# Twenty-eight tiles of a mean edge layer looked up on TensorE from a table copy in SBUF

## The reference

```python
h = x @ W + b
agg = segment_sum(h[col], row, num_segments=n)
deg = segment_sum(ones, row, num_segments=n)
return agg * where(deg > 0, 1 / deg, 0)[:, None]
```

## Time and profile before

| | us |
|---|---|
| runs of the kernel before: median of 3 (lowest to highest) | 5398.98 (5395.08 to 5399.3) |
| the profiled execution's own time | 5395.97 |
| its span, first to last instruction | 5394.1 |
| mean granted TensorE clock of the span | 0.896 |

### The profile page before, as it was taken

The page is one execution under the profiler, slowest core; times in us unless marked ns, Lnnn a source line. Parts: engine busy times, 40 slices in busy tenths (PEclk is TensorE's granted clock), DMA queues, the critical chain, the costliest instruction groups (busy, mean ns, idle before and its releaser), DMA issues. The chain is left out here.

```text
span 5394.1 us, 106431 instructions
## 1 busy us (share of the span) xinstructions
PE 4401.4 (82%) x24965; PEld 3546.0 (66%) x24965; DVE 3865.9 (72%) x8445; ACT 1994.5 (37%) x3783; POOL 3395.0 (63%) x3492
## 2 busy tenths in 40 slices
PE   5999999999895888888885655555556899999793
PEld 4888888888675888888884555555555566666431
DVE  5999999999764887888788544444446677877673
ACT  3666666666424655655554300000003000000370
POOL 2677777777414777777640477777773777777473
PEclk8999999999997988999897777777787999999796
DMA  6333333333234555555535333333335111111243
GB/s 199 115 105 103 103 104 103 104 105 102 79 117 110 135 127 126 129 125 129 123 84 158 111 110 109 109 109 109 107 104 162 39 40 40 38 35 29 61 114 109
DMA packets 452024, 555.48 MB, mean 103 GB/s; under 512 B 213168, under 2 KB 322148, under 8 KB 451552
## 3 DMA queue, kind: packets, MB, share of 16 engines
q0 software_dynamic: 154128, 374.88, 25.6%
q1 hardware_dynamic: 290585, 172.07, 11.8%
q10 hardware_dynamic: 6840, 3.36, 0.3%
HBM read 497.40 MB, written 59.40 MB: 103 GB/s over the span
## 5 line engine op out<-in xcount | busy, mean ns | idle before, releaser
L507 POOL DMA_INDIRECT l_rows<-tmp_tab,l_idx x832 | 882.2, 1060 | 376.2 <-issue 252.2
L1170 POOL DMA_INDIRECT l_rows<-tmp_tab,src_sb x832 | 791.8, 952 | 321.8 <-issue 236.1
L1890 POOL DMA_INDIRECT l_rows<-tmp_tab,src_sb x812 | 767.7, 945 | 253.0 <-issue 236.5
L1976 PE MATMUL l_psa<-l_sel,l_rows 128*128 128x128 f32 x3248 | 571.2, 348 | 413.2 <-issue 222.6
L1976 PEld LDWEIGHTS l_psa<-l_sel,l_rows 128*128 128x128 f32 x3248 | 529.9, 255 | 454.5 <-issue 256.2
L2128 POOL DMA_INDIRECT l_rows<-tmp_tab,src_sb x695 | 656.5, 945 | 235.5 <-issue 201.3
L805 PE MATMUL l_psw<-l_fw,l_ssp 128*128 128x256 f32 x3328 | 763.2, 382 | 0.0
L1916 DVE TENSOR_TENSOR acc<-acc,l_psa 128x256 f32 x832 | 350.9, 422 | 536.8 <-PE l_psa L1976 445.1
L805 PEld LDWEIGHTS l_psw<-l_fw,l_ssp 128*128 128x128 f32 x3328 | 616.0, 190 | 154.1 <-issue 77.3
L2239 PE MATMUL l_found<-l_tabs,l_hot 128*128 128x384 f32 (+1 forms) x1872 | 651.7, 502 | 0.0
L1490 PE MATMUL l_psa<-l_sel,l_rows 128*128 128x128 f32 x3328 | 597.7, 308 | 57.2 <-DVE acc L1390 55.4
(11 more groups left out here) (355 smaller groups left out, 7747.8 us busy)
## 6 DMA issues: line engine op xcount, KB each, us to landing
l_rows<-tmp_tab,src_sb POOLq DMA_INDIRECT x2339
l_edge<-in_edge_t SPq DMA_DIRECT2D x104, 256.0 KB
l_own<-tmp_tab SPq DMA_DIRECT2D x1280, 1.0 KB
l_own<-tmp_tab ACTq DMA_DIRECT2D x1280, 1.0 KB
l_own<-tmp_tab ACTq DMA_DIRECT2D x1280, 0.2 KB
l_own<-tmp_tab SPq DMA_DIRECT2D x1280, 0.2 KB
tmp_x<-n_X SPq DMA_DIRECT2D x39, 512.0 KB
n_X<-in_x SPq DMA_DIRECT2D x26, 512.0 KB
```

The lines of the kernel that those rows point to most:

```text
L507: nc.gpsimd.indirect_dma_start(out=rows[r][:, t, :], out_offset=None, in_=table[:, :], in_offset=bass.IndirectOffsetOnAxis(ap=idx[q][:, j: ...
L1170: nc.gpsimd.indirect_dma_start(out=rows[r][:, j, :], out_offset=None, in_=dram["tab1"][:, :], in_offset=bass.IndirectOffsetOnAxis(ap=sh["s ...
L1890: nc.gpsimd.indirect_dma_start(out=rows[g % ROWS][:, t, :], out_offset=None, in_=table[:, :], in_offset=bass.IndirectOffsetOnAxis(ap=sh["s ...
L1976: last = nc.tensor.matmul(by_tile(g)[0:n, t, k * P:(k + 1) * P], left[:, f:f + n], sel[b][:, t, :], start=True, stop=True)
```

## The change

The mean layer's edge stage becomes a function of its own, `edges_mean`. A copy of `tab2` (6.8 MB) is loaded into SBUF at the start of the stage by four DMAs on ACT's queue, into a region that is later used for `acc3` and `dinv_r`. 28 groups (one in seven, from group 14) have their last tile looked up on TensorE in place of a fetch by POOL, so POOL issues 784 fetches where it issued 812. With 256 columns for each block, seven candidates don't fit into one PSUM bank, so the look-up goes in four rounds of two, two, two and one block, over two banks. The rounds are issued ahead of groups g-6, g-5, g-4 and g-3. VectorE builds `hot` eight groups ahead, and after each round adds its candidates to the tile's rows with a mask, one instruction for each block; in program order these stand between the select and the adds of a step. To make room, `psa` goes from six PSUM banks to five, and TensorE's wait for it is now made twice in a group, for two tiles each.

The spreading of `dinv` on TensorE and ACT goes. The roots are written to memory as a row, and the fourth layer's edge stage reads that row into `dinv_r` on all 64 partitions, behind its table load on ACT's queue. The low and high bits of the indices are now worked out in the mean layer, and `edges_gcn` no longer writes `mix_row` or waits for it.

```diff
+    BY_ROW, PERIOD, FIRST, SLOTS = 10, 7, 14, 8
+    MIX = 8
+    BANKS_A = 5
+    LAG = 2
+    HIGHS = [-(-(-(-N // P) - j) // MIX) for j in range(MIX)]
+    ROUNDS = [(0, 2), (2, 4), (4, 6), (6, HIGHS[0])]
...
+    looks = [g + (g in by_row) for g in range(FIRST, GROUPS - 2, PERIOD)]
+    look_of = {g: n for n, g in enumerate(looks)}
+    asked = [GT - (g in by_row or g in look_of) for g in range(GROUPS)]
...
+    round_at = {g - 6 + r: (n, r) for n, g in enumerate(looks) for r in range(len(ROUNDS))}
...
+        bank_of = lambda g, t: (g * GT + t) // 2 % BANKS_A * 512 + t % 2 * D
...
+                sp.dma_start(deg_l[:, :], dram["deg_row"].rearrange("a (p t) -> (a p) t", p=P)).then_inc(deg_in, 16)
+                sp.dma_start(runs[:, :], dram["src_runs"][:, :]).then_inc(runs_in, 16)
+                sp.wait_ge(mix_done, 2)
+                sp.dma_start(dram["mix_row"].rearrange("a (p n) -> (a p) n", p=P), mix_f[:, :]).then_inc(mix_out, 16)
+                sp.wait_ge(roots, 1)
+                sp.dma_start(dram["dinv_row"].rearrange("a (p t) -> (a p) t", p=P), deg_l[:, :]).then_inc(roots_out, 16)
+                sp.wait_ge(mix_out, 16)
...
+                for t in range(0, NT, CHUNKS):
+                    act.dma_start(tabs[:, t:t + CHUNKS, :], table[t * P:(t + CHUNKS) * P, :].rearrange("(t p) n -> p t n", p=P)
+                                  ).then_inc(tabs_in, 16)
...
-                for c in range(CHUNKS):
-                    act.wait_ge(spread, c + 1)
-                    nc.scalar.activation(dinv_r[:, c * CN:(c + 1) * CN], psa[0:H3, (1 + c % 2) * CN:(2 + c % 2) * CN],
-                                         ACT.Copy).then_inc(roots, 1)
...
+                def choose(n, r):
...
+                    dve.wait_ge(found_done, n * len(ROUNDS) + r + 1)
+                    for h in range(lo, hi):
+                        dve.wait_ge(chosen, HIGHS[0] * n + h)
+                        part = found[:, at + (h - lo) * D:at + (h - lo + 1) * D]
+                        if h == 0:
+                            nc.vector.tensor_scalar(out, part, mask[n % 2][:, 0:1], None, ALU.mult).then_inc(chosen, 1)
                         else:
+                            nc.vector.scalar_tensor_tensor(out=out, in0=part, scalar=mask[n % 2][:, h:h + 1], in1=out,
+                                                           op0=ALU.mult, op1=ALU.add).then_inc(chosen, 1)
...
+                for g in range(GROUPS + LAG):
+                    if g < GROUPS:
+                        select(g)
+                    if g == 0:
+                        mixed_sources()
                     if g == LAG - 1:
                         degrees()
+                    if g + 8 in look_of:
+                        one_hots(look_of[g + 8])
+                    if g - 1 in round_at:
+                        choose(*round_at[g - 1])
                     if g >= LAG:
                         add(g - LAG)
...
+                    users = [j for j in range(MIX) if HIGHS[j] > lo]
+                    for j in users:
+                        top = min(hi, HIGHS[j])
+                        first = j + lo * MIX
+                        last = nc.tensor.matmul(found[:, k % 2 * 512:k % 2 * 512 + (top - lo) * D].rearrange("p (h n) -> p h n", n=D),
+                                                hot[n % 2][:, j, :], tabs[:, first:first + (top - lo - 1) * MIX + 1:MIX, :],
+                                                start=(j == users[0]), stop=(j == users[-1]))
+                    last.then_inc(found_done, 1)
...
+                    if g in round_at:
+                        look_up(*round_at[g])
                     pe.wait_ge(sel_done, g + 1)
                     pe.wait_ge(gathered[b], rows_due(g))
+                    if g in look_of:
+                        pe.wait_ge(chosen, HIGHS[0] * (look_of[g] + 1))
...
-                    pe.wait_ge(added, GT * (g + 1))
                     for t in range(GT):
+                        if t % 2 == 0:
+                            pe.wait_ge(added, g * GT + t + 2)
...
+                act.dma_start(dinv_r[:, :], dram["dinv_row"].broadcast_to([H3, NP])).then_inc(dinv_in, 16)
```

More of the change, by code:

```diff
@@ L1820, in edges_rows @@
+    table = dram["tab2"]
+    with Phase(nc, "l2") as ph:
+        rows = [ph.sb(f"rows{i}", [P, GT, D]) for i in range(ROWS)]
         sel = [ph.sb(f"sel{i}", [P, GT, P]) for i in range(ROWS)]
-        dinv_r, inv, last_edge, has, dinv_c = degree
-        deg_c = ph.sb("deg_c", [P, NT])
-        upto, upper, ends = ph.sb("upto", [P, P]), ph.sb("upper", [P, NT]), ph.sb("ends", [P, NT])
-        deg_in, acc_zero, cols_done, cols_in = ph.sem("deg_in"), ph.sem("acc_zero"), ph.sem("cols_done"), ph.sem("cols_in")
@@ L1825, in edges_rows @@
-        counted, ranked, rooted, spread, roots = (ph.sem(n) for n in ("counted", "ranked", "rooted", "spread", "roots"))
-        psa = ph.ps("psa", deep * GT * wide)
-        iota_ps = ph.ps("iota_ps", 512)[:, 0:P]
-        S = ph.sem
+        runs, mixed, mix_f = ph.sb("runs", [P, TILES], I32), ph.sb("mixed", [P, TILES], I32), ph.sb("mix_f", [P, TILES])
+        mix_b = ph.sb("mix_b", [P, SLOTS, P])
+        hot = [ph.sb(f"hot{i}", [P, MIX, P]) for i in range(2)]
+        mask = [ph.sb(f"mask{i}", [P, HIGHS[0]]) for i in range(2)]
@@ new lines, in edges_mean @@
+        deg_c, deg_l = ph.sb("deg_c", [P, NT]), ph.sb("deg_l", [P, NT])
+        upto, upper, ends = ph.sb("upto", [P, P]), ph.sb("upper", [P, NT]), ph.sb("ends", [P, NT])
+        own = [[ph.sb(f"own{h}{q}", [P, D]) for q in range(2)] for h in range(2)]
+        src_r = ph.sb("src_r", [1, 2, 2, P], I32)
+        psa = ph.ps("psa", BANKS_A * 512)
+        found = ph.ps("found", 1024)
+        consts = ph.ps("consts", 512)
+        iota_ps, at_ps = consts[:, 0:P], consts[:, P:P + MIX]
+        S = ph.sem
@@ L1835, in edges_rows, with fetch_rows @@
         win_done = S("win_done", ROWS)
[L1836 to L1840, removed]
+        added = S("added", BANKS_A * 2)
+        bank_of = lambda g, t: (g * GT + t) // 2 % BANKS_A * 512 + t % 2 * D
+        def fetch_rows(eng, h, between):
+            regs = [eng.alloc_register(f"l2_row{h}{i}") for i in range(16)]
             mine = [g for g, (k, i) in turn_of.items() if k == h]
@@ L1937, in _ @@
                 nc.vector.tensor_copy(iota_ps, sh["iota"][:, :]).then_inc(iota_in, 1)
-                dve.wait_ge(iota_in, 1)
-                for g in range(GROUPS):
-                    select(g)
+                nc.vector.scalar_tensor_tensor(out=at_ps, in0=sh["iota"][:, 0:MIX], scalar=float(P),
+                                               in1=sh["part"][:, 0:1].to_broadcast([P, MIX]),
+                                               op0=ALU.mult, op1=ALU.add).then_inc(iota_in, 1)
+                dve.wait_ge(iota_in, 2)
@@ L1948, in _, with look_up @@
-            @block.tensor
+            @block_.tensor
             def _(pe):
                 pe.wait_ge(cols_in, 1)
-                pe.wait_ge(deg_in, 16)
+                pe.wait_ge(deg_in, 32)
                 nc.tensor.matmul(psa[:, 0:NT], upto[:, :], deg_c[:, :], start=True, stop=True)
                 nc.tensor.matmul(psa[:, NT:2 * NT], sh["ones"][:, :], deg_c[:, :], start=True, stop=True).then_inc(counted, 1)
[L1954 to L1963, removed]
-                pe.wait_ge(ranked, 1)
+                pe.wait_ge(ranked, 1)
+                def look_up(n, r):
+                    lo, hi = ROUNDS[r]
+                    k = n * len(ROUNDS) + r
+                    if n == 0 and r == 0:
+                        pe.wait_ge(tabs_in, 16 * CT)
+                    pe.wait_ge(hot_done, n + 1)
+                    if r >= 2:
+                        pe.wait_ge(chosen, HIGHS[0] * n + ROUNDS[r - 2][1])
+                    elif n:
+                        pe.wait_ge(chosen, HIGHS[0] * (n - 1) + ROUNDS[r + 2][1])
+                    users = [j for j in range(MIX) if HIGHS[j] > lo]
[6 more added lines that the diff above has]
+                    last.then_inc(found_done, 1)
@@ L1971, in _, with edges_gcn @@
                         pe.wait_ge(row_in[h][i % 2], 16 * P * (i // 2 + 1))
-                    pe.wait_ge(added, GT * (g + 1))
                     for t in range(GT):
-                        left = rows[b][:, t, :] if t < asked[g] else own[h][i % 2]
-                        for k, (f, n) in enumerate(blocks):
-                            last = nc.tensor.matmul(by_tile(g)[0:n, t, k * P:(k + 1) * P], left[:, f:f + n], sel[b][:, t, :],
+                        if t % 2 == 0:
+                            pe.wait_ge(added, g * GT + t + 2)
+                        left = own[h][i % 2] if g in by_row and t == GT - 1 else rows[b][:, t, :]
+                        for k in range(KH):
+                            at = bank_of(g, t) + k * P
+                            last = nc.tensor.matmul(psa[:, at:at + P], left[:, k * P:(k + 1) * P], sel[b][:, t, :],
                                                     start=True, stop=True)
```

(2 more changed lines are left out.)

130 lines of the change are left out of this document (75 added, 55 removed).

## The result

The changed kernel takes 5487.44 us (median of 4 runs, 5486.76 to 5488.78). The kernel before, run beside it, takes 5397.58 us (5395.08 to 5399.3). The ratio is 1.0167 (95% interval 1.015 to 1.0185): 89.9 us slower. The forecast was 5493. One run of the kernel before, beside the last four kernels of the experiments, took 14463.26 us and is left out of the medians given there.

The account below looks back on a forecast made before the run. POOL bound the kernel before; TensorE was to bound the changed stage at 38.0 us a period, ending at 4149 against 4048.6. 5396 + 100 - 3 (fourth layer) = 5493 us, range 5400 to 5560.

Parts of the forecast that it names:

- The bound passes to TensorE: Mean layer's edge stage: seven groups with one look-up cost TensorE 35.0 us, more than POOL's 32.9.
- rival 3: Edge stage: POOL stays the bound and 28 saved fetches make the kernel faster, 5358 us; chance 0.05.
- VectorE's order: Edge stage: due adds queue behind masked adds, so TensorE waits; 12.75 us where alone it would take 10.1.
- rival 1: Edge stage: TensorE is the bound and VectorE keeps up; stage +13 us, kernel 5406; chance 0.15.
- The rounds with two groups between: Rest of each edge-stage period: three look-up rounds with two groups between take 25.2 us while VectorE catches up.
- change from look-up to groups: TensorE, edge stage: each such change costs 0.3 us, taken from the fourth layer's look-up.
- the start: Edge stage's opening: edits hidden under POOL's fetches, first round waits for group 7 and the table copy until 3076.
- What lies behind the last look-up's first round: End of the edge stage: 25.2 us for three rounds, 11.5 for groups to 203, 10.3 for four last groups.
- The -3 us of the fourth layer: Fourth layer: single-row DMAs start some 3 us earlier, shrinking TensorE's wait of 15.0 us; between -5 and +5.
- rival 2: Edge stage: TensorE's clock also falls in its pauses, 3.4 us a period, 95 us, giving 5588; chance 0.12.
- Rival 4: Edge stage: the copy slows fetches and makes single rows late, at most some tens of us; within a 0.08 remainder.

Follow-up runs that it names:

- e2_one_product: The changed kernel with only the first product of each look-up round made, the other seven of the first three rounds left out: 5371.01 us, ratio 0.9943.
- e1_adds_first: The changed kernel with VectorE's adds of two groups back put ahead of a round's masked adds: 5434.17 us, ratio 1.0057 to the kernel before.
- e6_both_every_7: The changed kernel with adds ahead of masked adds and the table copy issued later, still a look-up every seventh group: 5421.49 us, ratio 1.0039.
- e5_copy_later: The changed kernel with the table copy issued behind ACT's clear and roots, once the indices have landed: 5476.2 us, ratio 1.0139 to the kernel before.

## Why the prediction was right

**The bound passes to TensorE.** It did: 119.0 us of waits of POOL, TensorE busy 95.45 of 100 us at clock 1.00, look-up instructions 0.43 us apart. e2_one_product, which takes TensorE's work away, gives -32.6 and shows the value of a fetch that rival 3 rested on. The 131 ns for 512 columns that the Trainium skill gives in "TensorE: Matmul & The Clock Gate", section "Back-to-back issue gap", without naming an element type, did not hold for these f32 products: 7.03 us for 16 instructions at the full clock.

**VectorE's order.** The prediction followed one period and got 12.75 us from the third round's end to the next look-up; the trace has 12.9 (3595.18 to 3608.08). e1_adds_first shows that it is the order that does it. This was the term that split the forecast from rival 1: TensorE alone would have been +13 by the prediction's sum. With the order undone the period is 35.13, close to that rival's 35.0, but that is luck: the 35.0 hold 1.2 us of change-overs that do not exist (next paragraph), and e1_adds_first still waits 32.4 / 28 = 1.2 us a period for VectorE. Its time stays at +30.5, and the late start is only a part of that: e6_both_every_7, whose first round comes 46.1 us after POOL's first fetch where that of e1_adds_first comes after 58.7, still has +21.1. The rest is the period itself, 35.13 us where POOL's seven groups took 34.2.

**The mis-sized terms.** The rounds with two groups between were put at 25.2 us, with 0.3 us for each change from look-up to groups. They take 24.3 (2 x 8.65 + 7.0): there is no such change-over. The 0.3 was what was left between one pair of rows of the fourth layer, too little to take a constant from. That makes 37.23 us a period instead of 38.0, 27 x 0.77 = 21 us too much. The other way went the start: the first round came at 3085.0, not 3076 (bounds 3072 to 3081). I had laid the edits of the start under the cover of POOL's fetches and asked when the copy would land. I had not asked what waits behind the copy on its way, so that the degree rows and indices came late and held group 0 to 3065.08. From there the eight groups ahead of the first round take 19.9 us, 2.49 each, close to VectorE's step of 2.58. What lies behind the last look-up's first round was 46.3 us to TensorE's end (predicted 47.0). The end came at 4136.5 for 4149: 9.0 - 20.8 - 0.7 = -12.5 us.

**Behind the stage.** The -3 us of the fourth layer did not come. Its wait for single rows is 14.6 us (15.0 before):

```profile
PE l_psa L2343 <- DMA l_own<-tmp_tab: 14.6, 1, 14.6
```

SP's first loads from `mix_row` did go out sooner, 6.3 us after that stage's start where it was 12.9, but its single rows began 56.9 us after it where it was 54.9. That the loads ahead of them share the DMA engines with the 1.7 MB of `dinv_r` is the likely reason, which no run tested. The layer costs 0.5 us more than before. Two smaller terms were not in the sum: the last adds now end 4.7 us after TensorE's last group (2.2 before), and another 2.0 us pass until the fourth layer's first look-up. Altogether -12.5 + 3.5 + 2.5 + 2.0 = -4.5, and the spans of the profiled executions differ by 92.5 us for the 97 forecast. So the result is this close in part because two errors of 21 and 9 us had opposite signs.

**The other rivals.** The clock (rival 2) fell in two of the 27 periods and held in the rest. In most of them TensorE paused 0.55, 0.98 and 0.55 us between its groups, as in the period shown, and the granted clock stayed 1.00. In two periods the middle pause was longer, and the group behind it was slow; in the timeline of the kernel after:

```profile
3230.42 1.16 PE L2071 MATMUL l_psa<-l_sel,l_rows 128*128 128x128 f32 x8 [1.33 <-DVE acc L1946]
3232.12 3.66 PE L2071 MATMUL l_psa<-l_sel,l_rows 128*128 128x128 f32 x16 [0.55 <-DVE l_sel L1936]
...
3343.23 1.16 PE L2071 MATMUL l_psa<-l_sel,l_rows 128*128 128x128 f32 x8 [1.38 <-DVE acc L1946]
3344.94 2.93 PE L2071 MATMUL l_psa<-l_sel,l_rows 128*128 128x128 f32 x12 [0.55 <-DVE l_sel L1936]
```

The group took 3.66 us where it takes 2.05. The granted clock was 0.57 from 3232 to 3236 and 0.59 from 3344 to 3348, so for a part of each stretch at the lower of its two levels (1.2 GHz), and 1.00 in the four us before each. The two falls cost 2.0 and 1.5 us: one period took 39.02 us where most take 37.07, and two in a row took 75.66 where such a pair takes 74.14 elsewhere. So the rival was real in kind and 3.5 us in size, where it had put 95. In e1_adds_first, whose pauses are shorter (0.51 and 0.55 us around 3580), no stretch of 20 us from 3100 to 4040 shows less than 1.00. The Trainium skill, same page, section "A second HAM failure mode: psum-queue depth-cycling", tells of a kernel in which short idle stretches between groups that cycle through PSUM made the clock swing; here two periods show this and 25 do not. Rival 4, a copy that delays more than the start, was real in its kind: it is the 13 us of e5_copy_later, though not through slowed fetches.

## What to carry to other kernels

When work moves from a full engine to one that has room, write down one period for each engine in its own program order: the engine between the two, here VectorE at half load, decided 59 us by standing in front of a wait with due work behind it. Then choose how much to move by where the two periods meet: with the order and the start mended, one look-up in 8 groups wins 28.0 us and one in 7 loses 21.1. Give a large copy its place behind the small loads that the first result needs.

## What the runs showed of the hardware

In this kernel a small transfer paid for a large one on another engine's queue. The transfer of the degree row in the DMA issues (queue, kind, count, size, us from issue to landing), first before, then after:

```profile
l_deg_c<-tmp_deg_row SPq DMA_DIRECT2D x1, 26.0 KB, 6.5
```
```profile
l_deg_c<-tmp_deg_row SPq DMA_DIRECT2D x1, 26.0 KB, 30.0
```

It went out 0.01 us ahead of ACT's 6.8 MB copy and took 30.0 us for 6.5; with the copy moved behind it (e5_copy_later) it took 6.6. This agrees with the Trainium skill, "DMA: Bandwidth & Descriptors", section "Issuing engines are not separate DMA queues": transfers started by the scalar, sync or gpsimd engine run on the same 16 DMA engines and interleave. The price was not only in the landing: the next small issue held SP's queue for 20.16 us, and 4.49 with the copy moved.
